# Where VectorE takes the near neighbours' maxima during the second graph layer

## The chip, the cores and the metric

The kernel runs on one core of a Trainium2 chip. The metric is the device time of one execution in microseconds (us). Before the change it is 4166.41 us, the median of three runs that lie between 4166.37 and 4169.35 us.

## What is computed

Four graph layers over 8192 nodes of 128 features, all with the same dense 8192x8192 adjacency matrix (fp32, 256 MB), each on a layer-normalised and rectified copy `h` of `x`, and each added to `x`:

```python
h = relu(layernorm(x)); x = x + relu(rownorm(a*adj + (1-a)*I) @ h @ W0.T + b0)  # layer 0
h = relu(layernorm(x)); x = x + hyperbolic_mean(h @ W1, adj)                    # layer 1: adj @ (8192x129)
h = relu(layernorm(x)); t = h @ W2.T + b2
x = x + max(t[top_k(adj, 32)], axis=1)                                          # layer 2: a gather
h = relu(layernorm(x)); x = x + expmap(relu(log(coef(adj) @ h) @ W3 + b3))      # layer 3
```

A row of `adj` has some nine entries above zero. Layer 2 needs for each node the elementwise maximum over the rows of `t` that belong to its 32 largest entries, which is a gather and a maximum.

## The kernel before

The 8192 nodes are 64 tiles of 128. Everything is written out by hand, one instruction stream for each engine, with semaphores between them.

**First pass (layer 0).** `adj` is read once. TensorE transposes it and multiplies, the turned matrix is stored to `adj_turned`, and VectorE picks the neighbours of each row into lists `IDX`. A near list holds neighbours among the first 2048 nodes, a far list those among the rest. The lists of one tile have a common length, held in `CTL`.

**Second pass (layer 1, `turned_pass`), where the change lies.** TensorE works through eight supergroups s = 0 to 7 of eight tiles (1024 nodes) each. A supergroup is 32 steps k over loads of `adj_turned`. The sums of s stand in one of two sets of PSUM banks, by the parity of s. When TensorE is through with s:

- ScalarE takes the sums out (`take_sums(s)`, lines 710 to 716).
- VectorE and ScalarE then run the **chain** of s together (`l1_rows(s)` on both): some seventy small operations, each waiting for the one before. It finishes layer 1 for those 1024 nodes and normalises the result (`h2_ready`). On VectorE it begins at line 1164 and ends with two additions of the bias (line 1235), after TensorE has projected the two halves with `W2`.
- TensorE turns and projects the chain's result (`turn_h2`, line 538, and `project_h2`, line 548) inside supergroup s+1, at step k = 20 (after the first two chains) or k = 24 (after the others). Its queue is in order: if `h2_ready` is not there yet, it waits, and supergroup s+1 waits with it. The last chain is projected behind the pass.
- ScalarE stores the 1024 projected rows into `h_table` in DRAM.

**Near maxima.** Once the first two supergroups are in `h_table`, the near neighbours can be gathered. For each tile a = 0 to 63:

- GpSimd issues one indirect DMA for the list's first entry and one for each near neighbour (`gather`, line 422), each bringing 128 rows into one slot of the ring. There are two rings, by the parity of a. It starts tile a when VectorE has copied the list of a into `idx_now` (line 1109).
- VectorE (`near_tile(a)`) waits for the gathers, takes the maximum over the ring's slots into `GB` (line 1096), and copies the list of tile a+2.
- ScalarE stores the maximum into `base_rows` (`store_base`, line 767). `GB` has six places, so `near_tile(a)` also waits until the store of a-6 has landed.

Two tables of eight numbers say where VectorE does this. `NEAR_IN[s]` tiles are worked inside chain s, one at each of the places 2, 5, 8, 11, 13 and 15 (`NEAR_STEPS`) at which the generator `l1_rows` yields. `NEAR_AFTER[s]` tiles, and what is left of `NEAR_IN[s]`, are worked behind chain s:

```python
for n, _ in enumerate(l1_rows(s)):
    if n + 1 in NEAR_STEPS and todo:
        near_tile(a)
        a, todo = a + 1, todo - 1
for _ in range(todo + NEAR_AFTER[s]):
    near_tile(a)
```

ScalarE goes through the pass in this order:

```python
for s in range(NSG):
    take_sums(s)
    l1_rows(s)
    for a in range(stored, stored + NEAR_IN[s] + NEAR_AFTER[s]):
        store_base(a)
```

**Then.** With all of `h_table` stored, GpSimd gathers the far neighbours tile by tile, VectorE adds their maxima and finishes layer 2 (`far_tile`), and TensorE multiplies for layer 3 (line 610). A last part projects with `W3` and writes `out`.

Of the kernel before, what the change touches and what calls it, by code (L numbers as in the profile page):

```python
# [73 lines left out]
def build(nc, x, adj, alpha, w0, b0, w1, w2, b2, w3, b3, out):  # L74
# [10 lines left out]
    CHUNKS = NT // CT  # L85
    ROW = P + 1
    SPANS = [(0, 3), (3, 6), (6, 8)]
    NEAR_IN = [0, 0, 6, 6, 6, 6, 6, 2]
    NEAR_AFTER = [0, 4, 6, 6, 6, 6, 4, 0]
    NEAR_STEPS = (2, 5, 8, 11, 13, 15)  # L90
    GBS = 6
    assert NPC % SLOTS == 0 and CT == BPP and NSG == 8 and NEAR * PIECE == 2 * SGW and sum(NEAR_IN + NEAR_AFTER) == NT

# [14 lines left out]
    with ctx:  # L108
# [537 lines left out]
        def _(act):  # L646
# [118 lines left out]
            def store_base(a):  # L765
                act.wait_ge(base_ready, a + 1)
                nc.scalar.dma_start(base_v[a, :, :], GB[:, a % GBS, :]).then_inc(base_stored[a % GBS], 16)
# [65 lines left out]
# [5 lines that stand above are left out]
                stored += NEAR_IN[s] + NEAR_AFTER[s]  # L838

# [39 lines left out]
        def _(dve):  # L879
# [231 lines left out]
            def near_tile(a):  # L1111
                par = a % 2
                n = dve.value_load(CTL[0:1, 0, a:a + 1], min_val=1, max_val=HALFK)
                dve.wait_ge(near_gathered[par], FULL_A * (a // 2 + 1))
                dve.sem_inc(carrier["dve"], 1)
                if a >= GBS:
                    dve.wait_ge(base_stored[a % GBS], 16 * (a // GBS))
                reduce_ring(par, GB[:, a % GBS, :], n, CUTS_A, base_ready)
                stage_list(a + 2)
# [123 lines left out]
            def turned_pass():  # L1243
                a = 0
                for s in range(NSG):
                    todo = NEAR_IN[s]
# [6 lines that stand above are left out]
# [170 lines left out]
```

## Time and profile before

| | |
|---|---|
| median of three runs | 4166.41 us |
| the profiled execution, its own time | 4168.62 us |
| its span, first to last instruction | 4167.0 us |
| mean granted TensorE clock | 0.92 of full |
| TensorE busy (matmul) | 3415.7 us, 82% |
| VectorE busy | 2443.4 us, 59% |
| ScalarE busy | 1706.7 us, 41% |
| GpSimd busy | 1531.6 us, 37% |
| DMA | 1190 MB, mean 286 GB/s |

TensorE is the busiest over the whole span, but the shares are means over passes with different limits. The second pass lies between about 1841 and 2923 us of the span. The near gathers run from 2172 to 2882 us. The busy share of an engine in that stretch, and what its waits end on, have to be read there.

### The profile page before, as it was taken

Reading aid. Unit: us, or ns where it says so; the run is one execution under the profiler, and the core shown is the slowest. Engines: PE = TensorE matmul, PEld = TensorE weight load, DVE = VectorE, ACT = ScalarE, POOL = GpSimd, SP = SyncE. Lnnn points to the kernel's source line nnn. Section 1 sums busy time; section 2 is a strip of 40 time slices with the busy share of each in tenths; the row PEclk is TensorE's granted clock in tenths of the full one; section 3 lists DMA queues with packets and bytes.
Section 4 is the critical chain, followed back from the end, with each engine's and each line's share of the span. In section 5 each row is a group of like instructions: output and inputs, shape, how many; then the busy total and the mean of one; then the engine's idle time right before and its main releaser. Section 6 shows DMA issues by size and latency. Waiting matters only on the chain.

```text
span 4167.0 us, 75269 instructions
## 1 busy us (share of the span) xinstructions
PE 3415.7 (82%) x23492; PEld 2829.5 (68%) x23492; DVE 2443.4 (59%) x5921; ACT 1706.7 (41%) x4362; POOL 1531.6 (37%) x1850
## 2 busy tenths in 40 slices
PE   3989898989899998059999988892188989999892
PEld 2555555555555555059999988892188989999892
DVE  6999999999999999841113323333134434334334
ACT  2777777777777777121222112222111111111135
POOL 0111111111111111000016666674677777777720
PEclk9999999999999999579999999996599999999997
DMA  3988898988898898128889988893298999899971
GB/s 102 351 336 341 336 347 337 344 337 341 338 345 341 341 343 323 50 76 296 291 296 338 345 291 305 298 319 111 71 310 299 326 308 335 297 315 339 307 260 41
DMA packets 569449, 1190.43 MB, mean 286 GB/s; under 512 B 45182, under 2 KB 87103, under 8 KB 569087
## 3 DMA queue, kind: packets, MB, share of 16 engines
q1 hardware_dynamic: 416944, 814.20, 55.7%
q0 software_dynamic: 116096, 355.32, 22.9%
q10 hardware_dynamic: 36046, 16.82, 1.4%
q8 instruction: 136, 2.23, 0.2%
q14 instruction: 227, 1.85, 0.1%
HBM read 905.12 MB, written 281.05 MB: 285 GB/s over the span
## 4 chain that ended last, share of the span: by engine, by line
DVE 31%; issue 24%; PE 22%; POOL 12%; ACT 4%; DMA 3%; DVEq 2%; POOLq 1%; SPq 0%; ACTq 0%
DVE D L1049 12%; POOL D L422 12%; PE psT L574 9%; DVE D L1052 6%; PE psT L610 6%; PE psU L574 3%; DMA D<-h_table,idx_now 3%; PE psU L610 2%; ACT junk_rows L703 1%; DVEq L56 1%; DVE D L998 1%; DVE sm L923 1%; DVE D L1003 1%; DVE gmax L1096 1%; PE psX L492 0%
## 5 line engine op out<-in xcount | busy, mean ns | idle before, releaser
L422 POOL DMA_INDIRECT D<-h_table,idx_now x1324 | 1255.2, 948 | 1045.7 <-issue 929.4
L528 PE MATMUL psU<-ATS,HB 128*128 128x512 f32 x2048 | 1012.9, 620 | 123.6 <-ACT ATS L674 123.6
L610 PE MATMUL psT<-ATS,PIECES 128*128 128x129 f32 x6144 | 796.7, 281 | 173.5 <-ACT ATS L795 170.9
L610 PEld LDWEIGHTS psT<-ATS,PIECES 128*128 128x128 f32 x6144 | 751.6, 197 | 177.2 <-ACT ATS L795 174.0
L574 PE MATMUL psT<-HB,PIECES 128*128 128x129 f32 x6144 | 778.8, 277 | 32.4 <-DVEq L58 31.9
L574 PEld LDWEIGHTS psT<-HB,PIECES 128*128 128x128 f32 x6144 | 736.0, 194 | 32.9 <-DVEq L58 32.1
L409 POOL DMA_DIRECT2D adj_turned<-ATS x512 | 272.4, 532 | 1303.3 <-ACT ATS L674 876.3
L1052 DVE FIND_INDEX8 D<-D,PIECES 128x8 uint32<-128x512 f32 x1024 | 696.3, 686 | 0.0
L515 PEld LDWEIGHTS psT<-ident,PIECES 128*128 128x128 f32 x4096 | 490.2, 144 | 302.1 <-issue 234.0
L1049 DVE MAX8 D<-PIECES 128x8 f32<-128x512 f32 x1024 | 671.3, 677 | 2.3
L674 ACT ACTIVATE ATS<-psT 128x1024 f32<-128x1024 f32 x512 | 520.8, 1023 | 304.2 <-PE psT L515 158.6
L528 PEld LDWEIGHTS psU<-ATS,HB 128*128 128x128 f32 x2048 | 364.4, 198 | 399.3 <-issue 338.7
L515 PE MATMUL psT<-ident,PIECES 128*128 128x128 f32 x4096 | 546.7, 279 | 21.1 <-DMA PIECES<-in_adj 19.5
L1265 DVE TENSOR_TENSOR HB<-psT,HB 128x387 f32<-128x387 f32 x240 | 123.4, 555 | 469.9 <-PE psU L610 469.8
L780 ACT ACTIVATE junk_rows<-X 128x128 f32<-128x128 f32 x64 | 19.8, 310 | 873.8 <-issue 821.1
L685 ACT ACTIVATE psX<-PIECES 128x512 f32<-128x512 f32 x512 | 303.5, 593 | 90.1 <-DVEq L58 90.1
L610 PE MATMUL psU<-ATS,PIECES 128*128 128x129 f32 x2048 | 318.5, 279 | 0.0
L574 PE MATMUL psU<-HB,PIECES 128*128 128x129 f32 x2048 | 314.5, 277 | 0.0
L1096 DVE TENSOR_REDUCE gmax<-D 128x128 f32<-128x1664 f32 (+3 forms) x64 | 209.9, 3280 | 162.8 <-DMA D<-h_table,idx_now 161.8
L685 ACT ACTIVATE psY<-PIECES 128x512 f32<-128x512 f32 x512 | 301.3, 588 | 0.0
L1096 DVE TENSOR_REDUCE GB<-D 128x128 f32<-128x896 f32 (+2 forms) x64 | 116.0, 1813 | 312.0 <-DMA D<-h_table,idx_now 286.1
L610 PEld LDWEIGHTS psU<-ATS,PIECES 128*128 128x128 f32 x2048 | 276.1, 196 | 0.0
(258 smaller groups left out, 2201.1 us busy)
## 6 DMA issues: line engine op xcount, KB each, us to landing
PIECES<-adj_turned SPq DMA_DIRECT2D x512, 1024.0 KB
PIECES<-in_adj SPq DMA_DIRECT2D x256, 1024.0 KB
adj_turned<-ATS POOLq DMA_DIRECT2D x512, 512.0 KB, 6.6
D<-h_table,idx_now POOLq DMA_INDIRECT x1324
h_table<-AGG ACTq DMA_DIRECT2D x8, 512.0 KB
base_rows<-GB ACTq DMA_DIRECT2D x64, 64.0 KB, 6.5
D<-base_rows ACTq DMA_DIRECT2D x64, 64.0 KB
D<-h_table ACTq DMA_DIRECT2D x64, 64.0 KB
```

Source lines behind the costliest of these rows:

```text
L409: pool.dma_start(turned[bass.ds(g, 1), k, :, :], AT[k % NAT]).then_inc(pair_stored[k % NAT], 16)
L422: pool.indirect_dma_start(ring[par][:, slot, :], None, near_table if done is near_gathered else table, bass.IndirectOffsetOnAxis(ap=idx_no ...
L515: last = nc.tensor.transpose(psT[k % 2][:, b * GROUP + r * P:b * GROUP + (r + 1) * P], pieces[(k // 2) % SLOTS][:, r, x0:x0 + P], ident[:, :])
L528: last = nc.tensor.matmul(psA, H[:, j, :], AT[k % NAT][:, b * GROUP:(b + 1) * GROUP], start=(j == 0), stop=(j == NT - 1))
L574: last = nc.tensor.matmul(acc(s % 2, r), wide[q % SLOTS][:, b, r * P:(r + 1) * P], HB[:, j, :], start=(j == 0 and opens(r)), stop=(j == NT ...
L610: last = nc.tensor.matmul(acc(m % 2, r), wide[q % SLOTS][:, b, r * P:(r + 1) * P], Hc[c % 2][:, jj, :], start=(jj == 0 and opens(r)), stop ...
L674: nc.scalar.activation(AT[k % NAT], psT[k % 2][:, :], ACT.Copy).then_inc(pair_copied, 1)
L685: st.mark(nc.scalar.activation(junk[r % 2][:, :], pieces[c % SLOTS][:, r, :], ACT.Copy, accum_out=rs_part[:, r, c:c + 1]))
L1049: found.append(sc.mark(v.max(cand[:, r, c, :], pc[:, r, :])))
L1052: sc.mark(v.max_index(cidx[:, r - 1, c, :], cand[:, r - 1, c, :], pc[:, r - 1, :]))
L1096: v.tensor_reduce(out, ring[par][:, 0:cuts[0] + 1, :].rearrange("p k f -> p f k"), AX.X, ALU.max).then_inc(done, 1)
L1265: last = v.tensor_tensor(sums, acc_rows(m % 2, n), sums, ALU.add)
```

## The change

Only the two tables change. The sum over both stays at 64 tiles.

```diff
     SPANS = [(0, 3), (3, 6), (6, 8)]
-    NEAR_IN = [0, 0, 6, 6, 6, 6, 6, 2]
-    NEAR_AFTER = [0, 4, 6, 6, 6, 6, 4, 0]
+    NEAR_IN = [0, 0, 6, 6, 6, 6, 3, 0]
+    NEAR_AFTER = [0, 5, 8, 8, 8, 8, 0, 0]
     NEAR_STEPS = (2, 5, 8, 11, 13, 15)
```

Tiles by supergroup go from 0, 4, 12, 12, 12, 12, 10, 2 to 0, 5, 14, 14, 14, 14, 3, 0. Every tile keeps its order, its gathers, its maximum and its store. ScalarE's loop of `store_base` follows the same sums. Nothing else is touched.

## Rows read from the trace of the kernel before

**Rows 1.** The page's 40 slices: busy tenths of GpSimd.
```profile
POOL 0111111111111111000016666674677777777720
```
**Rows 2.** Waits, 2172 to 2882 us: total us, times, longest.
```profile
ACT junk_rows L710 <- DVE GB L1096: 392.1, 6, 75.5
...
POOL D L422 <- DVE idx_now L1109: 110.5, 35, 21.8
...
PE psX L538 <- ACTq L58: 48.4, 4, 16.3
```
**Rows 3.** VectorE's timeline, chain 3 and behind it: start, us, form, idle.
```profile
2364.21 1.71 DVE L1096 TENSOR_REDUCE GB<-D 128x128 f32<-128x896 f32 x1 [7.62 <-DMA D<-h_table,idx_now]
...
2370.91 0.17 DVE L1164 TENSOR_SCALAR sm<-DEN 128x8 f32<-128x8 f32 x1 [4.91 <-ACT AGG L716]
...
2375.06 1.71 DVE L1096 TENSOR_REDUCE GB<-D 128x128 f32<-128x896 f32 x1 [0.97 <-DVE sm L930]
...
2385.85 1.94 DVE L1096 TENSOR_REDUCE GB<-D 128x128 f32<-128x1024 f32 x1 [1.17 <-issue]
...
2408.60 1.68 DVE L1096 TENSOR_REDUCE GB<-D 128x128 f32<-128x896 f32 x1 [0.97 <-DVE AGG L1226]
...
2412.86 0.20 DVE L1230 RECIPROCAL sm<-sm 128x8 f32<-128x8 f32 x1 [2.51 <-ACT sm L740]
...
2430.18 0.69 DVE L1235 TENSOR_TENSOR AGG<-psY,bias 128x512 f32<-128x512 f32 x1 [7.79 <-PE psY L548]
...
2431.04 1.72 DVE L1096 TENSOR_REDUCE GB<-D 128x128 f32<-128x896 f32 x1 [0.17 <-issue]
...
2494.37 1.93 DVE L1096 TENSOR_REDUCE GB<-D 128x128 f32<-128x1024 f32 x1 [8.55 <-DMA D<-h_table,idx_now]
...
2501.29 0.17 DVE L1164 TENSOR_SCALAR sm<-DEN 128x8 f32<-128x8 f32 x1 [4.90 <-ACT AGG L716]
```
**Rows 4.** GpSimd's timeline, three gathers of line 422.
```profile
2221.03 0.94 POOL L422 DMA_INDIRECT D<-h_table,idx_now  x1 [0.30 <-issue]
...
2298.13 0.94 POOL L422 DMA_INDIRECT D<-h_table,idx_now  x1 [21.80 <-DVE idx_now L1109]
...
2433.63 0.94 POOL L422 DMA_INDIRECT D<-h_table,idx_now  x1 [12.70 <-DVE idx_now L1109]
```
**Rows 5.** Line 1096's near maxima: duration min/median/max, first and last start, forms.
```profile
L1096 DVE TENSOR_REDUCE GB<-D x64: 1658/1717/2160, 2185.0 to 2885.1; 128x128 f32<-128x896 f32 x37, 128x128 f32<-128x1024 f32 x22, 128x128 f32<-128x1152 f32 x5
```
**Rows 6.** VectorE's timeline: chain 1, starts of chains 2 and 6, chain 7.
```profile
2079.58 0.17 DVE L1164 TENSOR_SCALAR sm<-DEN 128x8 f32<-128x8 f32 x1 [25.85 <-ACT AGG L716]
...
2115.66 0.20 DVE L1230 RECIPROCAL sm<-sm 128x8 f32<-128x8 f32 x1 [5.24 <-ACT sm L740]
...
2224.71 0.17 DVE L1164 TENSOR_SCALAR sm<-DEN 128x8 f32<-128x8 f32 x1 [4.90 <-ACT AGG L716]
...
2761.88 0.17 DVE L1164 TENSOR_SCALAR sm<-DEN 128x8 f32<-128x8 f32 x1 [4.94 <-ACT AGG L716]
...
2869.50 0.25 DVE L1164 TENSOR_SCALAR sm<-DEN 128x8 f32<-128x8 f32 x1 [4.73 <-ACT AGG L716]
...
2912.19 0.20 DVE L1230 RECIPROCAL sm<-sm 128x8 f32<-128x8 f32 x1 [5.23 <-ACT sm L740]
```
**Rows 7.** TensorE's timeline: two projections, last matmuls of layer 1, first of layer 3.
```profile
2281.07 0.60 PE L538 MATMUL psX<-ident,AGG 128*128 128x128 f32 x4
...
2805.38 1.12 PE L538 MATMUL psX<-ident,AGG 128*128 128x128 f32 x4 [9.35 <-ACTq L58]
...
2835.49 0.61 PE L574 MATMUL psU<-HB,PIECES 128*128 128x129 f32 x4
...
3008.35 2.95 PE L610 MATMUL psT<-ATS,PIECES 128*128 128x129 f32 x12 [86.60 <-ACT ATS L795]
...
3013.64 0.61 PE L610 MATMUL psU<-ATS,PIECES 128*128 128x129 f32 x4
```

**Rows 8.** The stores of `GB`, issue to landing.
```profile
DMA to landing us min/median/max: 1.7/6.5/11.7
```

## The prediction

> **What bounds the kernel now.** The change touches only the second pass, so I read that stretch and left the kernel's shares aside. The page's slices came first: GpSimd's digits jump from 0 to 6 or 7 as soon as the near gathers begin, and stay there to the end of the pass and beyond [rows 1]. It does nothing there but issue gathers. Then the waits of that stretch [rows 2]. The reader is to see three things. ScalarE spends 392.1 us in six waits before line 710, the first instruction of `take_sums`, and each ends on a near maximum of VectorE. GpSimd waits 110.5 us in all for lists. TensorE waits 48.4 us for chains that are late.
>
> The timeline of VectorE shows why [rows 3]. The last near maximum behind chain 2 ends at 2364.21 + 1.71 = 2365.92, and chain 3 begins 4.99 us later, at 2370.91. The last one behind chain 3 ends at 2496.30, and chain 4 begins 4.99 us later. So it is at chains 2 to 7. The code gives the reason: ScalarE's `take_sums(s+1)` is queued behind the `store_base` of every near tile that belongs to supergroup s. The next chain therefore doesn't wait for TensorE but for the last near tile, and each tile put behind a chain delays the next chain by what that tile takes.
>
> What does a tile take? GpSimd issues a gather in 0.94 us with 0.30 us ahead of the next [rows 4]; I count 1.25 us. The forms of the maxima tell how many slots each has: 37 have 7, 22 have 8, 5 have 9 [rows 5], which is 259 + 176 + 45 = 480 gathers, 7.5 a tile, 9.4 us. The maximum itself takes 1.7 to 2.2 us and lies beside the gathers of the other ring. So between chains the pace is GpSimd's issue, and VectorE mostly waits for gathers.
>
> In the chain the pace is another. Four maxima are taken there, not six (2375.06, 2385.85, one more, 2408.60): `l1_rows` yields twelve times, so places 13 and 15 never come, and the other two stand right behind the chain (from 2431.04). Both rings are then full and no list is staged, and GpSimd stands until 2433.63, after 12.70 us idle [rows 4]. This hole comes once a chain, and more tiles behind the chain don't fill it.
>
> **The cost, step by step.** I count the gathers that lie between GpSimd's restart behind a chain and the next chain's start.
>
> 1. *Supergroup 1, one more tile.* Tile 4 (nine gathers) moves ahead of chain 2. Its last gather is issued at 2221.03 [rows 4]. From there to the maximum I take 7.0 us, as behind chain 3 (44 gathers from 2433.63, the last at 2433.63 + 43 x 1.25 = 2487.4, the maximum at 2494.37); the maximum takes some 2.2, and then come the 4.99: chain 2 starts at about 2235 instead of 2224.71 [rows 6]. The work that hides this is TensorE's: chain 2's projection was made at 2281.07 without a wait [rows 7]. A chain with four maxima has its result some 43.5 us after its start, so 2279 to 2280 now, and TensorE reaches step 24 at 2281 all the same. GpSimd's restart at 2298.13 hangs on TensorE's step and stays. Cost nothing; bounds 0 and +11.
>
> 2. *Supergroups 2 to 5, two more tiles each.* Before, 6 tiles follow the restart, with 45, 44, 44 and 43 gathers, 176 in all. After, 8 tiles follow: tiles 11 to 18, 25 to 32, 39 to 46 and 53 to 60, with 60, 60, 62 and 58, which is 240 (8 x 7.5 = 60 is the mean too). One tile in each is the one that step 1 brought forward. That is 64 gathers more: 64 x 1.25 = **+80.0 us** on the start of chain 6, from 2761.88 [rows 6] to about 2841.9. Nothing hides them: TensorE, which was already waiting before step 24, waits longer by as much in each. Queued behind VectorE's longer wait is the chain, behind it TensorE's step 24 and all that follows. Bounds: the gap between the last issue and the chain's start was 12.7 us behind chain 3 (2433.63 + 44 x 1.25 = 2488.6, to 2501.29), and about 12 elsewhere. The chains' own lengths differ by 2.5 us with whether the first maximum's gathers are late. Four stages give -8 to +8.
>
> 3. *Supergroup 6, three tiles instead of ten.* The three are taken inside chain 6, at places 2, 5 and 8, and nothing is left behind it. The next chain then waits for TensorE. Before, chain 6 began at 2761.88 and TensorE's supergroup 7 ended at 2835.49 + 0.61 = 2836.10 [rows 6, 7]: 74.2 us, since TensorE had been waiting for chain 6 before step 24, as it will again. Add 4.7 for `take_sums` without a store ahead of it: chain 7 begins 78.9 us after chain 6. Before it was 2869.50 - 2761.88 = 107.6. That is **-28.7 us**. The fourth maximum that chain 6 loses gives nothing: places 8 and 11 lie beside ScalarE's work (step 4). Bounds -32 to -26.
>
> 4. *Supergroup 7, no maxima in the last chain.* With two, at places 2 and 5, line 1230 comes at 2912.19 - 2869.50 = 42.7 us; chain 1, with none, has it at 2115.66 - 2079.58 = 36.1 [rows 6]. Chain 3 with four has it at 41.95 [rows 3], so the first two cost 3.3 each and the others nothing. This chain has no cover: the last rows of `h_table`, and so every far gather, wait for it. **-6.6 us**; bounds -7 and -5.
>
> Sum: +80.0 - 28.7 - 6.6 = **+44.7 us**. What follows, the far gathers and layer 3, starts later by that and is otherwise the same work. The sum is made against the profiled execution (4168.62 us, span 4167.0); the median of the runs shown is 2.2 us below its time. 4166.4 + 44.7 = 4211.1, and I say **4211 us**.
>
> In short, before, 62 tiles had to be through when chain 7 began, and the last ten of them filled 107.6 us in which TensorE needed 79. After, 61 must be through before chain 6, one supergroup earlier.
>
> **A rule that speaks against it.** TensorE's waits before step 24 grow by the 20 us of the longer stage, from 9.35 us at supergroup 7 to about 30. After the 9.35 us the four transposes took 1.12 us, against 0.60 without a wait [rows 7], so the clock had fallen to its lower level. The rest of supergroup 7 ran from 2805.38 to 2836.10, 30.7 us, nearly all of it at the upper one. After 86.60 us without work the first 12 matmuls of layer 3 took 2.95 us, and from 3013.64 on four took the same 0.61 us as at the end of the pass [rows 7]. So a long wait was paid back in about 5 us, as a short one was. The Trainium skill ("TensorE: Matmul & The Clock Gate", the section on HAM oscillation) says that repeated waits between bursts throw TensorE back to 1.2 GHz each time and that a kernel can lose much of its rate so. By that rule the rest of supergroup 7 could stay slow; by the rows it doesn't. That is the second rival.
>
> **The rivals.**
>
> - *The gathers fit into GpSimd's holes, and the change gains.* GpSimd stands 110.5 us over the pass [rows 2], more than the 80 of the added gathers. Were they to fall there, chain 6 would begin as before and only steps 3 and 4 were left: 4166.4 - 35.3 = 4131 us. It decides where the restart comes ahead of the chain's end. Against it: the hole is there because the two rings are full while VectorE waits for the projection, and the added tiles stand behind it. 2 in 100. With the near tiles hidden altogether, so that only step 4 counted, it would be 4166.4 - 6.6 = 4160; the 392.1 us of ScalarE speak against it. 1 in 100.
> - *TensorE stays slow after the longer wait.* All of 30.7 us at the lower clock is up to +29: 4240 us. It decides where the clock doesn't come back within the eight steps. Against it stands the restart after 86.60 us. 3 in 100.
> - *The ring of six stores binds.* With eight tiles in a run, the seventh and later wait for the store of six before. Stores are issued as soon as a maximum is there, six tiles are 56 us, and they land within 11.7 us [rows 8]. It decides where a store takes longer than that. At 6 us a stage: 4235 us. 3 in 100.
> - *The change does nothing,* because the tiles per stage don't count and the two ends cancel: this needs step 2 to cost 35 and not 80, so 0.55 us a gather. GpSimd's 0.94 us of work for each forbids it. 2 in 100.
>
> **The range.** My forecast has 89 in 100. Its terms, all at their ends, give +25 and +64 (4191 and 4230), but they won't all lie at one end. I take 4198 to 4225. Outside is what remains of the forecast's own error, and the rivals, together less than 2 in 10. A measurement of this kernel can tell about 0.2% (8 us) from no change. The chances are 0.03 for faster by over that, 0.02 for within, and 0.95 for slower.
>
> **What the profile after should show.** Chains 2 to 7 start near 2235, 2390, 2540, 2692, 2842 and 2921 us. Six near maxima stay in or right behind the chains 2 to 5, and eight behind those. The interval from the last near maximum to the next chain is again 5.0 us at chains 2 to 6, while chain 7 follows TensorE's last matmul of the pass instead. TensorE's waits before line 538 grow from 48.4 us to about 130 us. The two additions of chain 7 end at about 2967 instead of 2922.5. Should chain 3 start at 2371, step 2 is wrong; should chain 7 take 53 us from its start to its end, step 4. If the time between chain 6 and chain 7 isn't near 79 us, step 3 is.

## The result, and the profile after

The changed kernel takes 4214.81 us (median of four runs, 4212.35 to 4222.9). The kernel before takes 4166.53 us in the same comparison. The ratio is 1.0119, with a 95% interval from 1.0106 to 1.0132: 48 us slower, where 44.7 were forecast. The profiled execution took 4217.07 us with a span of 4215.4 us, so what follows is read from an execution 2.3 us above the median.

VectorE's timeline after the change, around the starts of the chains (start us, duration us, line, form, idle before and who ended it), answers to [rows 3, 6]:

```profile
2229.25 2.15 DVE L1096 TENSOR_REDUCE GB<-D 128x128 f32<-128x1152 f32 x1 [10.00 <-DMA D<-h_table,idx_now]
2236.39 0.17 DVE L1164 TENSOR_SCALAR sm<-DEN 128x8 f32<-128x8 f32 x1 [4.91 <-ACT AGG L716]
...
2382.20 1.72 DVE L1096 TENSOR_REDUCE GB<-D 128x128 f32<-128x896 f32 x1 [7.00 <-DMA D<-h_table,idx_now]
2388.91 0.17 DVE L1164 TENSOR_SCALAR sm<-DEN 128x8 f32<-128x8 f32 x1 [4.91 <-ACT AGG L716]
...
2538.62 0.36 DVE L1164 TENSOR_SCALAR sm<-DEN 128x8 f32<-128x8 f32 x1 [5.05 <-ACT AGG L716]
...
2691.32 0.17 DVE L1164 TENSOR_SCALAR sm<-DEN 128x8 f32<-128x8 f32 x1 [4.91 <-ACT AGG L716]
...
2833.80 1.72 DVE L1096 TENSOR_REDUCE GB<-D 128x128 f32<-128x896 f32 x1 [5.74 <-DMA D<-h_table,idx_now]
2840.51 0.17 DVE L1164 TENSOR_SCALAR sm<-DEN 128x8 f32<-128x8 f32 x1 [4.91 <-ACT AGG L716]
...
2918.91 0.17 DVE L1164 TENSOR_SCALAR sm<-DEN 128x8 f32<-128x8 f32 x1 [18.26 <-ACT AGG L716]
...
2955.34 0.20 DVE L1230 RECIPROCAL sm<-sm 128x8 f32<-128x8 f32 x1 [5.23 <-ACT sm L740]
...
2964.93 0.69 DVE L1235 TENSOR_TENSOR AGG<-psY,bias 128x512 f32<-128x512 f32 x1 [2.92 <-PE psY L548]
```

Chains 2 to 6 each start 5.0 to 5.1 us behind the end of the last near maximum, as before: 2382.20 + 1.72 = 2383.92, then 2388.91, 4.99 later. Chain 7 has no near maximum ahead of it. VectorE stood for 18.26 us there and was released by ScalarE's `take_sums`, which had waited for TensorE.

The waits from 2172 to 2942 us (total us, times, longest) answer to [rows 2]:

```profile
ACT junk_rows L710 <- DVE GB L1096: 344.9, 4, 92.3
...
PE psX L538 <- ACTq L58: 126.4, 4, 32.8
ACT junk_rows L710 <- PE psU L574: 108.0, 2, 89.8
POOL D L422 <- DVE idx_now L1109: 86.1, 35, 12.7
```

TensorE's waits for chains grew from 48.4 to 126.4 us. Of ScalarE's two waits put down to TensorE, the one of 18.2 us at chain 7 is truly TensorE's. The one of 89.8 us ahead of chain 6 is not: it ended at 2835.93 us, 0.4 us behind the last near maximum (2833.80 + 1.72 = 2835.52), when TensorE had long been done. So five chains still wait for near maxima and one for TensorE. GpSimd's waits for lists fell by 24 us. Two holes account for it: the one behind chain 2, which was 21.80 us before [rows 4] and is 12.03 now, because tile 4's maximum moved ahead of the chain and one list more was ready, and the one behind chain 6, which was 13.51 us and is gone, as no near tile is left to gather there. The other three stayed at 11 to 13 us. The one behind chain 3 is 11.99 us, against 12.70:

```profile
2451.93 0.94 POOL L422 DMA_INDIRECT D<-h_table,idx_now  x1 [11.99 <-DVE idx_now L1109]
```

TensorE's timeline at supergroup 7 answers to [rows 7]:

```profile
2884.61 1.11 PE L538 MATMUL psX<-ident,AGG 128*128 128x128 f32 x4 [31.07 <-ACTq L58]
2885.52 2.79 PE L574 MATMUL psT<-HB,PIECES 128*128 128x129 f32 x12
...
2888.61 1.50 PE L574 MATMUL psT<-HB,PIECES 128*128 128x129 f32 x12
...
2913.61 0.61 PE L574 MATMUL psU<-HB,PIECES 128*128 128x129 f32 x4
```

After a wait of 31.07 us, 12 matmuls took 2.79 us, and 3 us later 12 took 1.50 again. The granted clock is 0.55 from 2884.6 to 2888.6 us, so TensorE was at its lower level (1.2 GHz) for most of that stretch, and 1.00 from there to 2914.2, the upper level (2.4 GHz). From the transposes to the last matmul of the pass it is 2914.22 - 2884.61 = 29.6 us, where it was 30.7.

A part of the 48 us lies behind the pass. The pass ends 2965.62 - 2922.47 = 43.2 us later in the profiled executions, of which 1.3 came from ahead of chain 1 (it starts at 2080.84 us, against 2079.58), where the two kernels are the same. Layer 3 took 1.9 us more, and the last projection 3.1. The stretch of that projection, before and then after (us, busy us and instructions of TensorE's matmuls and loads, VectorE, ScalarE, GpSimd; granted clock; DMA):

```profile
4082.00:4128.00 46.00, 27.71 (x184) 23.42 (x184) 15.02 (x17) 36.47 (x132) 0.00 (x0) 0.90 0.00 1
```
```profile
4127.00:4176.00 49.00, 33.05 (x184) 28.10 (x184) 15.05 (x17) 36.06 (x130) 0.00 (x0) 0.75 0.00 1
```

The same 184 matmuls at a granted clock of 0.75 instead of 0.90. TensorE works there in short bursts. The code of this part is the same in all fourteen traces of this case, and in a stretch of 46 us of it (from 86 to 40 us ahead of the last instruction) the granted clock lies anywhere between 0.73 and 0.92. With one and the same kernel, e3 and f3, it is 0.91 and 0.79. So the 3.1 us don't belong to the change.

### The profile page after: what moved, and what is told of

The parts are those of the page before. It is cut to its first block, busy times and chain, and to the rows that moved or that the text cites. A ratio compares the mean times of both kernels' runs of the same rounds, so it can differ in the third digit from the quotient of the medians.

```text
span 4215.4 us, 75270 instructions
## 1 busy us (share of the span) xinstructions
PE 3415.3 (81%) x23492; PEld 2827.7 (67%) x23492; DVE 2444.8 (58%) x5921; ACT 1706.8 (40%) x4362; POOL 1531.3 (36%) x1850
## 4 chain that ended last, share of the span: by engine, by line
DVE 31%; issue 25%; PE 18%; POOL 14%; DMA 4%; ACT 4%; DVEq 2%; POOLq 1%; SPq 0%; ACTq 0%
POOL D L422 14%; DVE D L1049 12%; PE psT L574 9%; DVE D L1052 6%; DMA D<-h_table,idx_now 4%; PE psU L574 3%; PE psT L610 3%; ACT junk_rows L703 1%; DVEq L56 1%; PE psU L610 1%; DVE D L998 1%; DVE sm L923 1%; DVE gmax L1096 1%; DVE D L1003 1%; PE psX L492 0%
```

## The experiments

The first nine runs landed on two chips on which the kernel before takes 5213 to 5258 us, the last three on one on which it takes 4170.4. All comparisons are with the kernel before on the same chip. So no edit of one part alone was measured where the prediction holds; there, the split into steps rests on the traces before and after and on h1 to h3.

### One part alone: the last chain freed (e1, f1)

```diff
-    NEAR_IN = [0, 0, 6, 6, 6, 6, 6, 2]
-    NEAR_AFTER = [0, 4, 6, 6, 6, 6, 4, 0]
+    NEAR_IN = [0, 0, 6, 6, 6, 6, 6, 0]
+    NEAR_AFTER = [0, 4, 6, 6, 6, 6, 6, 0]
```

> One part of the change alone: the two maxima (tiles 62 and 63) leave the last chain and stand behind chain 6; everything else as before. Theory (the next chain waits for the last near tile, whose pace is the issue of gathers): their 8 + 9 gathers x 1.25 us put chain 7 21.2 us later, the last chain is 6.6 us shorter, sum +14.6, about 4181 us. Rival (the near tiles behind a chain are hidden, only the last chain counts): -6.6, about 4160 us.

> The same edit as in e1 (tiles 62 and 63 leave the last chain and stand behind chain 6), on another chip if there is one: in the first four runs the kernel before itself took 5258 us, because TensorE got its instructions slowly while gathers ran, and the near tiles weren't what it waited for. Where the kernel before takes 4166 us, the theory (the next chain waits for the last near tile, its pace is the issue of gathers) gives 17 gathers x 1.25 = +21.2 and -6.6, about 4181 us; the rival (only the last chain counts) -6.6, about 4160 us.

Measured: 5252.70 against 5257.90 us (ratio 0.9992, 0.9981 to 1.0004), and 5205.89 against 5212.98 (0.9984, 0.9970 to 0.9998). The last chain had its line 1230 36.3 us after its start in both. The first difference, -5.2 us, isn't clear of no change; the second is -7.1 us. Both are near what the rival said, and the 21.2 us of the theory are missing. But on these chips the near tiles aren't what the next chain waits for. The timelines of f1 show why, first TensorE's:

```profile
2180.84 1.50 PE L574 MATMUL psT<-HB,PIECES 128*128 128x129 f32 x12
...
2184.68 0.27 PE L574 MATMUL psT<-HB,PIECES 128*128 128x129 f32 x1 [1.14 <-issue]
...
2188.92 0.38 PE L574 MATMUL psT<-HB,PIECES 128*128 128x129 f32 x1 [1.75 <-issue]
```

and GpSimd's first near gather:

```profile
2173.72 1.19 POOL L422 DMA_INDIRECT D<-h_table,idx_now  x1 [486.84 <-issue]
```

Nine microseconds after the first gather TensorE falls from 12 matmuls in 1.50 us to one at a time, 0.7 to 3.5 us apart, with no wait that the profile shows. It recovers at about 2243 us, when GpSimd stands still (from 2235 to 2265), and falls again when it goes on. On the chip of the first comparison TensorE runs at its full rate beside the gathers. A stretch of the kernel before there, and then one of f1, each 40 us long with the same work of GpSimd (columns as above):

```profile
2180.00:2220.00 40.00, 40.00 (x361) 40.00 (x360) 7.85 (x8) 0.00 (x0) 30.25 (x33) 1.00 0.99 343
```
```profile
2190.00:2230.00 40.00, 5.63 (x15) 4.31 (x15) 5.87 (x6) 0.00 (x0) 30.26 (x32) 0.50 0.19 57
```

That is 361 matmuls against 15. So here a supergroup lasts about TensorE's work plus much of the gathers' time, wherever the gathers stand. Chains 2 to 6 of f1 start 29 to 41 us behind the last near maximum, where they started 5.0 behind it on the first chip. That TensorE "got its instructions slowly", as the expectation has it, is what the rows look like; why they come slowly no row says.

### Tiles moved within the pass, and place 12 (e2, e3, f3)

```diff
 # e2
-    NEAR_AFTER = [0, 4, 6, 6, 6, 6, 4, 0]
+    NEAR_AFTER = [0, 4, 8, 6, 6, 6, 2, 0]
 # e3, f3
-    NEAR_STEPS = (2, 5, 8, 11, 13, 15)
+    NEAR_STEPS = (2, 5, 8, 11, 12, 15)
```

> Two tiles are moved from behind chain 6 to behind chain 2; 62 tiles are still through before chain 7. Theory: chains 3 to 6 start 18 to 19 us later, chain 7 at the same time as before (from chain 6 to chain 7 then 89 us, more than the 79 that TensorE needs), so no change: 4166 us within 4. Rival (what counts is TensorE's waits, and each us of them is lost): the wait before step 24 grows by 18 to 19 us in supergroup 4, so about 4185 us.

> A fifth maximum is taken inside each of chains 2 to 6, at place 12, where VectorE waits for the projection; the tiles per supergroup stay as before. Theory (GpSimd stands because both rings are full until the chain ends): one list more is staged ahead of the hole, so a tile's gathers, 7 or 8 x 1.25 = 9 to 10 us, fall into it in each of five chains, and a maximum may hold the projection up by 1 to 2 us each. Sum -40 to -45, about 4124 us. Rival (the holes don't matter, more work in a chain only lengthens it): 0 to +9, 4166 to 4175 us.

> The same edit as in e3 (a fifth maximum inside each of chains 2 to 6). Where the kernel before takes 4166 us, the theory (GpSimd stands because both rings are full until the chain ends) gives -40 to -45, about 4124 us; the rival (the holes don't matter, a longer chain does) 0 to +9.

Measured: e2 5260.69 us, ratio 1.0007 (0.9993 to 1.0020). That is the number of the theory, but it says little, since on this chip the next chain doesn't wait for a near maximum anyway (30 to 40 us lie between them). e3 5258.05 us, 0.9996 (0.9980 to 1.0012), and f3 5218.46, 1.0007 (0.9994 to 1.0021): no gain. But the edit didn't fill the hole either: GpSimd's waits for lists from 2172 to 3380 us come to 528.9 us in f3, and to 527.1 in f1, which takes nothing at place 12. While TensorE is starved, GpSimd stands up to 80 us at a time, because the end of the chain hangs on TensorE's projection. Whether place 12 gives its 40 us where the kernel before takes 4166 us was not measured.

### One gather more a tile (e4, f4)

```diff
-        FULL_A = 16 * (1 + HALFK)
+        FULL_A = 16 * (2 + HALFK)
...
+                    gather(par, RING - 1, 0, near_gathered, 16)
                     for k in range(-1, COMMON_A):
```

> Each near tile issues one gather more, into a free slot; the maxima read the same slots as before, so VectorE's work is the same. It measures the price of a gather in its place. Theory: the six tiles of a chain lose theirs in the hole before GpSimd's restart, and the four behind chain 1 theirs in TensorE's cover; the 28 tiles gathered between a restart and the next chain's start cost 28 x 1.25 = +35, about 4201 us. Rival A (GpSimd's issue is one queue in which every gather counts): 62 x 1.25 = +77, about 4244 us. Rival B (VectorE or the landing sets the pace, not the issue): +0 to +5, 4166 to 4171 us.

> The same edit as in e4 (each near tile issues one gather more into a free slot, the maxima are the same). Where the kernel before takes 4166 us, the theory gives 28 tiles x 1.25 = +35, about 4201 us; rival A (every gather counts, wherever it lies) +77, about 4244 us; rival B (VectorE or the landing sets the pace) 0 to +5.

Measured: 5364.57 us, ratio 1.0201 (1.0179 to 1.0224), and 5318.89, 1.0200 (1.0171 to 1.0229): +106.7 and +105.9 us, above every forecast. For 64 gathers that is 1.66 us each, more than the 1.25 us that GpSimd takes to issue one. In the traces of f1 and f4, whose tables are alike in supergroups 2 to 5, the time from chain 2 to chain 6 is 868.0 and 940.1 us, which is 1.5 us for each of the 48 gathers more. That fits a TensorE that loses its time beside every gather; why it is more than the time of the issue isn't shown.

### A version meant to be better (f6)

```diff
-    NEAR_IN = [0, 0, 6, 6, 6, 6, 6, 2]
-    NEAR_AFTER = [0, 4, 6, 6, 6, 6, 4, 0]
-    NEAR_STEPS = (2, 5, 8, 11, 13, 15)
+    NEAR_IN = [0, 0, 6, 6, 6, 6, 6, 0]
+    NEAR_AFTER = [0, 4, 6, 6, 6, 6, 6, 0]
+    NEAR_STEPS = (2, 5, 8, 11, 12, 13)
...
                     v.tensor_tensor(AGG[...], psY[...], group_bias(1), ALU.add).then_inc(pj_taken, 1)
+                    if u == 2 * first:
+                        yield
```

> A fifth and a sixth maximum inside each of chains 2 to 6 (places 12 and 13, the latter a new yield between the two additions of the bias), 12 tiles at each of the supergroups 2 to 6, none in the last chain. Theory: without holes 12 tiles take 12 x 7.5 x 1.25 = 112 us, less than TensorE's 117 for a supergroup, so the chains follow TensorE and chain 7 starts near 2795 instead of 2869.5: -75 and -6.6, about 4085 to 4095 us. Rival (gathers lie on the path whatever the order, as the count before chain 7 rises from 62 to 64): about 4181 us as in f1. Rival (maxima beside the projection hold it up by their 2 us each): 4105 to 4115 us.

Measured: 5190.08 us, ratio 0.9952 (0.9935 to 0.9969), 22.9 us faster. It is the only version that beat the kernel before on its chip by more than 0.2%. Some 7 us of it are the last chain's (f1). The rest was won ahead of chain 7, which starts at 3299.95 us, against 3317.30 in f1. As place 12 alone gave nothing (f3), that points to place 13, or to the two together; place 13 wasn't tried by itself. Where the kernel before takes 4166 us it wasn't run.

### The whole change on a slow chip (g1)

> The whole change once more, on whatever chip this is. If the kernel before takes 4166 us here: +45 to +48, as recorded. If it takes 5200 to 5260, as on the two chips of the first eight runs, TensorE gets hardly an instruction while gathers run, so that the pass lasts TensorE's work plus the gathers' time wherever the gathers stand. Theory for that case: the cost of steps 2 and 3 is gone, only the shorter last chain is left, 0 to -10 us (ratio 0.998 to 1.000). Rival (the near tiles set the chains' starts there too, as the change's 64 gathers behind restarts say): +45, ratio 1.009.

Measured: 5230.00 us against 5213.62, ratio 1.0042 (1.0026 to 1.0058), +16.4 us. Both expectations failed. The stretches of the pass, in f1 from the start of chain 2 to that of chain 3, and then in g1 the same:

```profile
2257.00:2477.00 220.00, 137.13 (x1043) 130.82 (x1043) 43.13 (x108) 29.16 (x89) 86.00 (x90) 0.76 0.55 186
```
```profile
2268.00:2506.00 238.00, 137.12 (x1037) 129.92 (x1036) 46.05 (x110) 28.76 (x89) 98.24 (x103) 0.75 0.53 175
```

TensorE's instructions are the same but for a few records, and 13 gathers more make the stretch 18 us longer. An estimate: at the 361 matmuls in 40 us of the first chip the 1043 are 116 us of work, and 90 gathers of 1.25 us are 112, together 228 against 220 measured; for g1 it is 115 + 129 = 244 against 238. From chain 2 to chain 7 it is 1059.2 us in g1 and 1060.4 in f1: in the middle of the pass nothing is lost or won. Chain 2 itself starts 10.8 us later in g1 (2267.7 against 2256.9). It doesn't wait for tile 4's maximum, which ended 40 us before; it waits for TensorE, and the nine gathers of tile 4 (11 us) are nine more that TensorE stands beside. The theory had put this at nothing. The pass ends 9.7 us behind that of f1 (3373.58 and 3363.86), and f1 is 7.1 us below the kernel before, so the trace accounts for some 3 us of the 16.4. The rest stays open. The profiled execution of g1 (5215.01 us) lies 15 us below its median and that of f1 15 us above, and layer 3 behind the pass, the same work in both, takes 1644.4 us in g1 and 1661.9 in f1 from the first to the last matmul of line 610. A difference of 16 us is no more than that part varies by from one execution to another.

### TensorE taken out of the pass (h1, h2, h3)

To test the theory of the prediction without starvation, nearly all matmuls of the second pass are left out: eight remain at the first step of a supergroup, and one transpose at each of the others, so layer 1 isn't computed. Loads, waits, gathers, maxima, stores and chains stay.

```diff
-                        for b in range(2):
-                            j = 2 * k + b
-                            for r in range(TSG):
-                                last = nc.tensor.matmul(acc(s % 2, r), ..., start=..., stop=...)
+                        if k == 0:
+                            for r in range(TSG):
+                                last = nc.tensor.matmul(acc(s % 2, r), ..., start=opens(r), stop=closes(r))
+                        else:
+                            last = nc.tensor.transpose(acc(s % 2, TSG - 1)[:, 0:P], ..., ident[:, :])
                         last.then_inc(piece_multiplied, 1)
```

h1 has this with the tables of before, h2 with those of the change, h3 is h1 with the gather more of e4.

> The tables of before, with nearly all matmuls of the second pass left out: eight at a supergroup's first step, then one transpose a step, so that starved TensorE can't set the pace of the chains; loads, waits, gathers, maxima and chains are all there. Theory (the next chain waits for the last near tile, the pace is 1.25 us a gather): chains 2 to 7 start near 2225, 2350, 2475, 2600, 2724 and 2828 us, each 5.0 us behind the last near maximum, and the last chain's line 1230 is 42.7 us behind its start. Rival (loads or landings set the pace here): intervals of about 100 us or less, and chains that start without a near maximum ahead.

> The same with the tables of the change. Theory: chains start near 2236, 2381, 2526, 2674, 2816 and 2878 us, so chain 6 is 92 us later than with the tables of before (nine tiles, as TensorE's cover for the first is gone), chain 7 is 51 us later, the last chain 6.6 us shorter, and the pass ends 44 us later, though TensorE has almost nothing to do. Rival (the loss came from TensorE's longer waits and its clock): the pass ends within 10 us of the one with the tables of before.

> The tables of before, few matmuls, and one gather more for each near tile with the same maxima. Theory: with hardly a hole left, most of the gathers count: chain 7 starts 35 to 45 us later (about 28 tiles behind restarts and the ones in the chain that are on the path too), so +1.25 us for each of 28 to 36 tiles. Rival A (one queue, every gather counts): +77 us. Rival B (VectorE or the landings set the pace): 0 to +5 us.

These three landed on the chip of 4170.4 us. Measured: h1 4030.01, h2 4080.87, h3 4081.55 us. All six chains 2 to 7 of h1 start 4.99 or 5.00 us behind a near maximum. VectorE's timeline of h1 (its lines are shifted by one):

```profile
2624.11 1.66 DVE L1097 TENSOR_REDUCE GB<-D 128x128 f32<-128x896 f32 x1 [7.03 <-DMA D<-h_table,idx_now]
2630.77 0.17 DVE L1165 TENSOR_SCALAR sm<-DEN 128x8 f32<-128x8 f32 x1 [4.91 <-ACT AGG L717]
...
2722.83 1.66 DVE L1097 TENSOR_REDUCE GB<-D 128x128 f32<-128x896 f32 x1 [7.11 <-DMA D<-h_table,idx_now]
2729.48 0.23 DVE L1165 TENSOR_SCALAR sm<-DEN 128x8 f32<-128x8 f32 x1 [4.76 <-ACT AGG L717]
...
2772.13 0.20 DVE L1231 RECIPROCAL sm<-sm 128x8 f32<-128x8 f32 x1 [5.23 <-ACT sm L741]
```

and of h2:

```profile
2720.19 1.66 DVE L1097 TENSOR_REDUCE GB<-D 128x128 f32<-128x896 f32 x1 [6.98 <-DMA D<-h_table,idx_now]
2726.85 0.17 DVE L1165 TENSOR_SCALAR sm<-DEN 128x8 f32<-128x8 f32 x1 [4.91 <-ACT AGG L717]
...
2788.97 0.17 DVE L1165 TENSOR_SCALAR sm<-DEN 128x8 f32<-128x8 f32 x1 [9.22 <-ACT AGG L717]
...
2825.36 0.20 DVE L1231 RECIPROCAL sm<-sm 128x8 f32<-128x8 f32 x1 [5.23 <-ACT sm L741]
```

The absolute starts came some 80 to 100 us earlier than expected, as chains 0 and 1 no longer wait for TensorE and I had left them where they were. The intervals between the chains of h1 are 127, 120, 120, 120 and 99 us, up to 5 shorter than expected: TensorE now projects at once, and GpSimd's holes at the chains' ends are 3 to 5.5 us long instead of 12. The differences are what was asked. With chain 1 at 2016.08 and 2017.97 us as the zero (1.9 us apart), chain 6 starts 94.2 us later in h2 (forecast 92), chain 7 57.6 (51), and the last chain is 42.65 and 36.39 us long (6.3 shorter; 6.6). The medians are 50.9 us apart (44). In the pass the change costs 94.2 - 36.6 - 6.3 = 51.3 us, against 41.9 in the whole kernel: step 1's tile isn't hidden here (11.6 us), step 2 is 82.6 instead of 77.4, and the freed supergroup 6 gives back 36.6 instead of 29.2 (chain 7 follows chain 6 after 62.1 us instead of 98.7). So the like medians (50.9 and 48.3) are in part chance. But the rival, that the loss came from TensorE's waits and its clock, is out: TensorE has next to no work in this pass, and the loss is there all the same.

h3 starts chain 7 at 2776.88 us, with chain 1 at 2017.81: 45.7 us later than h1, just above the theory's upper end. The whole kernel takes 48.0 us more in the profiled executions and 51.5 in the medians. GpSimd's waits for lists from 2060 to 2850 us, in h1 and in h3 (total us, times, longest):

```profile
POOL D L422 <- DVE idx_now L1110: 53.3, 40, 5.5
```
```profile
POOL D L422 <- DVE idx_now L1111: 18.4, 29, 2.3
```

The 62 gathers more ahead of chain 7 are 77.5 us of issue. 34.9 of them went into waits that GpSimd had anyway, which leaves 42.6, against 45.7 measured; the other 3 us aren't explained. So neither does every gather count (rival A), nor is it free (rival B): here a gather costs its 1.25 us except where GpSimd stood.

## Why the prediction was right, step by step

- *What bounds the pass.* Right, and shown: the 5.0 to 5.1 us from near maximum to chain hold at chains 2 to 6, all but the freed one. h1 and h2 show that it is not TensorE, and h3 that the price is the issue of a gather. All this holds on the chips where the kernel before takes 4166 to 4170 us, and not on the other two.
- *Step 1, the ninth tile free.* Right where TensorE covers it: chain 2 at 2236.39 us (forecast 2235), the restart of GpSimd where it was. Without TensorE's work the cover is gone, and the tile costs 11.6 us (2156.73 - 2143.23, less 1.9). The 10.8 us of g1 have another cause, as said there.
- *Step 2, +80.0.* Measured 2840.51 - 2761.88 - 1.3 = +77.4 us on chain 6, with the 1.3 us from ahead of chain 1 taken off. The chains started at 2236, 2389, 2539, 2691 and 2841 us, within 2 us of those foretold. Of the missing 2.6 us, 2.2 are chain 5's own length: its line 1230 came 43.92 us after its start before and comes after 41.76 now. The bounds name such a difference.
- *Step 3, -28.7.* Measured 78.40 - 107.62 = -29.2.
- *Step 4, -6.6.* Measured 36.43 - 42.69 = -6.3.
- *The sum.* 77.4 - 29.2 - 6.3 = 41.9 to the last line 1230 of the pass, against 44.7. The profiled executions are 48.4 us apart. The other 6.5 are the 1.3 from ahead of chain 1 and some 5 from what I had called "otherwise the same work". It is the same work, but with a clock in the last projection that differs between executions. So the terms are right to within 3 us each, and that their sum lies as near to 48 as it does is in part luck: the steps came out 2.8 us too high, and 6.5 us that no step has came on top. The two fastest runs after (4212.35 and 4212.55) are 46 us above the median of before, nearer the sum than the median is.
- *The range.* Its bounds were added up wrongly. The lower ends give 0 + 72 - 32 - 7 = +33 and the upper ends 11 + 88 - 26 - 5 = +68, not +25 and +64. The range that was taken, 4198 to 4225, leaves out a part of what the right upper end allows; it holds the result.
- *The clock after a wait.* The rows after agree with the rows before: after waits of 30 to 33 us the lower clock lasted some 3 to 6 us, no longer than after waits of 9 to 16 us. The Trainium skill ("TensorE: Matmul & The Clock Gate", the section on HAM oscillation) has TensorE fall back after each such gap, and the trace agrees: it did so four times in the second pass, with 1.11 or 1.12 us for the four transposes each time. That the work behind the gap would stay slow was the prediction's reading, and not what the section says; the rest of supergroup 7 took 29.6 us, with 30.7 before.
- *The rivals.* Gathers in the holes: no, as four holes of 11 to 13 us stayed and chain 6 moved by the 77.4 us. The slow TensorE: no, by the 29.6 us. The ring of six stores: no near maximum waits for a store in the trace after.

## What to carry to other kernels

When work on a side queue stands between the stages of a chain, ask which of its items must be through before the last stage starts, and not how many it has. Here both tables hold 64 tiles, and moving them one stage earlier put 77 us ahead of chain 6, of which the freed end gave back 35.5. Price such items by what paces them (here 1.25 us a gather) minus the holes they fall into, and see first that a hole is open at their place.

## What was not expected of the hardware

On both chips of the first nine experiments TensorE nearly stood while GpSimd issued indirect DMAs: 28 matmul records in 70 us in one stretch of e1, 49.17 us of which GpSimd was busy, at a granted clock of 0.52:

```profile
2400.00:2470.00 70.00, 10.02 (x28) 7.55 (x27) 11.10 (x12) 0.00 (x0) 49.17 (x52) 0.52 0.23 66
```

The same kernel takes 4170 us on one chip and 5213 and 5258 on the others, and the order of the near tiles that costs 1.2% where it takes 4166 us costs 0.4% there. The single matmuls come at distances near multiples of 0.7 us: in f1 they start at 2184.68, 2185.41, 2186.10, 2186.82, 2188.92 and 2191.74 us. The profile calls the idle time "issue", so it names no wait, and what holds the instructions back was not found.
